# A graph layer on one core: segment sums in four column tiles with the fp32 one-hots stationary, an unrolled program, and layer norm statistics on VectorE

## What is computed

```python
N_NODES = 6250; F_X = F_E = F_OUT = 128; HIDDEN = 512      # 106,250 edges
h = jnp.maximum(_layernorm(x, axis=-1), 0.0)
agg = jax.ops.segment_sum(edge_attr, receivers, num_segments=N_NODES)   # receivers = dst, sorted
y = jnp.concatenate([agg, h], axis=1)
return x + jax.nn.relu(y @ W1 + b1) @ W2 + b2
```

## Time and profile before

| | |
|---|---|
| time, median of three runs | 326.34 us (325.3 to 327.11) |
| span of the profiled execution, first to last instruction | 320.9 us |
| what lies around that span, if the profiled execution took the median | 5.4 us |
| PE busy | 293.4 us, 91% |
| DVE busy | 287.6 us, 90% |
| POOL, ACT busy | 186.4 us and 127.8 us |
| bytes moved | 62.29 MB, mean 194 GB/s |

### The profile page before, as it was taken

The page is one execution under the profiler, slowest core; times in us unless marked ns, Lnnn a source line. Parts: engine busy times, 40 slices in busy tenths (PEclk is TensorE's granted clock), DMA queues, the critical chain, the costliest instruction groups (busy, mean ns, idle before and its releaser), DMA issues.

```text
span 320.9 us, 10106 instructions
## 1 busy us (share of the span) xinstructions
PE 293.4 (91%) x3270; PEld 289.1 (90%) x3270; DVE 287.6 (90%) x576; ACT 127.8 (40%) x430; POOL 186.4 (58%) x212
## 2 busy tenths in 40 slices
PE   1428999999999999999999999999999999999971
PEld 1327999999999999999999999999999999999961
DVE  5998999999999999999999999999999999993310
ACT  4140234443343543444444344354344443435240
POOL 4485374664676577577567567657756756742011
PEclk9999999999999999999999999999999999999997
DMA  6973657666666776775766666677586577400000
GB/s 199 390 276 93 219 157 236 229 213 210 221 215 219 217 241 189 235 253 149 290 223 200 216 222 209 214 229 252 168 267 236 158 257 237 140 3 16 17 18 27
DMA packets 30624, 62.29 MB, mean 194 GB/s; under 512 B 2042, under 2 KB 8936, under 8 KB 30608
## 3 DMA queue, kind: packets, MB, share of 16 engines
q1 hardware_dynamic: 29202, 60.79, 58.0%
q10 hardware_dynamic: 1406, 1.30, 1.2%
HBM read 58.88 MB, written 3.20 MB: 193 GB/s over the span
## 4 chain that ended last, share of the span: by engine, by line
PE 82%; issue 8%; DVE 4%; DMA 2%; POOL 1%; DVEq 0%; SPq 0%; POOLq 0%; ACT 0%
PE bank L833 21%; PE bank L790 19%; PE bank L847 13%; PE bank L804 9%; PE bank L802 9%; PE bank L803 9%; DMA hidden<-in_dst 2%; PE bank L814 2%; DVE low L234 1%; DVE rem L231 1%; POOL outrow L371 1%; DVE onehot L585 0%; DVE relT L647 0%; DVEq L627 0%; DVE colB L661 0%
## 5 line engine op out<-in xcount | busy, mean ns | idle before, releaser
L802 PE MATMUL bank<-onehot_h,edges 128*128 128x48 bf16 (+1 forms) x535 | 95.3, 233 | 3.7 <-DVE low L234 1.9
L804 PE MATMUL bank<-onehot_h,low 128*128 128x48 bf16 (+1 forms) x535 | 96.8, 237 | 0.0
L803 PE MATMUL bank<-onehot_h,rem 128*128 128x48 bf16 (+1 forms) x535 | 96.7, 235 | 0.0
L790 PE MATMUL bank<-onehot,edges 128*128 128x48 f32 x600 | 78.3, 280 | 4.7 <-DVE base_tab L678 4.0
L234 DVE TENSOR_TENSOR low<-rem 128x640 bf16<-128x640 f32 x84 | 82.4, 981 | 0.0
L790 PEld LDWEIGHTS bank<-onehot,edges 128*128 128x128 f32 x600 | 77.1, 203 | 5.0 <-issue 4.9
L231 DVE TENSOR_TENSOR rem<-edges 128x640 f32<-128x640 f32 x84 | 79.4, 945 | 0.0
L580 DVE TENSOR_TENSOR onehot_h<-relT_h,iota_h 128x240 bf16<-128x240 bf16 x107 | 73.7, 688 | 1.3 <-DVE base_tab L678 0.9
L802 PEld LDWEIGHTS bank<-onehot_h,edges 128*128 128x128 bf16 (+1 forms) x535 | 62.8, 117 | 5.5 <-issue 4.4
L495 ACT ACTIVATE hidden<-bank,b_col 128x256 f32<-128x256 f32 (+1 forms) x100 | 41.4, 467 | 63.9 <-PE bank L833 63.9
L804 PEld LDWEIGHTS bank<-onehot_h,low 128*128 128x128 bf16 (+1 forms) x535 | 62.4, 117 | 0.0
(11 more groups left out here) (79 smaller groups left out, 489.1 us busy)
## 6 DMA issues: line engine op xcount, KB each, us to landing
edges<-in_edge_attr SPq DMA_DIRECT2D x48, 640.0 KB, 4.1
edges<-in_edge_attr SPq DMA_DIRECT2D x23, 960.0 KB, 5.1
out_rows<-outrow SPq DMA_DIRECT2D x24, 128.0 KB, 1.7
xs<-in_x SPq DMA_DIRECT2D x21, 128.0 KB, 3.7
w<-in_L_gnn_W ACTq DMA_DIRECT2D x1, 512.0 KB
xs<-in_x ACTq DMA_DIRECT2D x1, 384.0 KB, 4.5
hidden<-in_dst SPq DMA_DIRECT2D x1, 320.0 KB, 3.5
edges<-in_edge_attr SPq DMA_DIRECT2D x1, 320.0 KB
```

The costliest lines, as they stand in the source:

```text
L790: ins = nc.tensor.matmul(sums_ps, edges[0:kp, slot, g * F:(g + 1) * F], onehot[0:kp, PLAIN.index(k), g, :], start=(g == 0), stop=(g == G - 1))
L802: nc.tensor.matmul(sums_ps, high[0:kp, cols], hot, start=(g == 0), stop=False)
L803: nc.tensor.matmul(sums_ps, middle[0:kp, cols], hot, start=False, stop=False)
L804: ins = nc.tensor.matmul(sums_ps, low[0:kp, i, cols], hot, start=False, stop=(g == G - 1))
```

## The change

The sums are made the other way round. The one-hot is now the stationary operand, 32 nodes wide, and the edges are the moving one, so a matmul gives 32 nodes by 128 features. A chunk has 384 edges (3 per partition), and four chunks form a round (`ROUND`, 1536 edges, 70 rounds with the remainder): chunk t of a round writes PSUM partitions 32t to 32t+31 of one bank. No edge is split any more; each of the 12 matmuls of a round is fp32. The sums come out untransposed, so ACT copies them to SBUF once a block (`copy_sums`), PE turns them (`turn_sums`, one transpose a round) and DVE adds four windows of 32 columns a round into `aggT` (`add_sums`). Blocks take 4, 3, 3, 3, 2 ... rounds, 65 in blocks 1 to 23. The layer norm's mean and variance come from two batch-norm instructions on DVE (`stats`), POOL makes the reciprocal root (`spread`), DVE adds `b2` (`add_b2`) and finishes the output rows straight from PSUM (`finish`). No engine has a loop on the way through the blocks.

```diff
-G = 5
+G = 3
 CHUNK = P * G
-W = 48
-SC = 7
+W = 32
+TILES = 4
+ROUND = TILES * CHUNK
+RING = 8
...
@@ POOL
+            def spread(b):
+                pool.wait_ge(stats_ready, b + 1)
+                nc.gpsimd.tensor_scalar(var[0:w, par, :], meanvar[0:w, par, :, 1], 1e-5, None,
+                                        ALU.add).then_inc(var_ready, 1)
...
+                nc.gpsimd.tensor_tensor(rstd[0:w, par, :], var[0:w, par, :], power[0:w, :], ALU.pow).then_inc(pow_ready, 1)
@@ ACT, the loop over blocks
+            for k in range(NB):
+                h_out(k)
+                if k >= 1:
+                    round_agg(k - 1, (k - 1) % 2, k - 1, chunks_by(k - 1))
+                copy_sums(k)
+                if k + 2 < NB:
+                    normalise(k + 2)
...
+                if k >= 1:
+                    relu(k - 1, (k - 1) % 2, k - 1)
@@ DVE
+            def stats(b):
+                for j in range(2):
+                    nc.vector.bn_stats(halves[0:w, par, j, :], xs[0:w, b, j * F:(j + 1) * F]).then_inc(halves_ready, 1)
...
+                for j in range(2):
+                    ins = nc.vector.bn_aggr(meanvar[0:w, par, j, :], halves[0:w, par, j, :])
+                ins.then_inc(stats_ready, 1)
+            def add_sums(k):
+                dve.wait_ge(sums_turned, k + 1)
+                for i, r in enumerate(ROUNDS[k]):
+                    cs = chunks_of(r)
+                    _, bases = nc.values_load_multi_w_load_instructions(
+                        base_tab[0:1, r * TILES:r * TILES + len(cs)], engines=[dve.engine], min_val=0,
+                        max_val=N - 1, skip_runtime_bounds_check_because="clamped when written")
+                    for j, c in enumerate(cs):
+                        if c:
+                            dve.wait_ge(agg_added, c)
+                        win = aggT[:, bass.ds(bases[j], W)]
+                        at = i * F + j * W
+                        nc.vector.tensor_tensor(win, turn_ps[:, at:at + W], win, ALU.add).then_inc(agg_added, 1)
+            for k in range(NB):
+                if k >= 1:
+                    add_sums(k - 1)
+                rest_of_h(k)
+                if k >= 1:
+                    rest_of_agg(k - 1, (k - 1) % 2, k - 1)
+                if k >= 3:
+                    finish(k - 3, (k - 3) % 2, k - 3)
+                if k + 2 < NB:
+                    stats(k + 2)
...
+                if k + 1 < NB:
+                    for r in ROUNDS[k + 1]:
+                        build(r)
+                    add_b2(k + 1)
@@ PE
+            def sum_rounds(k):
...
+                        for g in range(G):
+                            for t in range(TILES):
+                                e = t * G + g
+                                ins = nc.tensor.matmul(sums_ps[t * W:(t + 1) * W, cols], onehot[:, hots, e, :],
+                                                       edges[:, slot, e * F:(e + 1) * F], start=(g == 0),
+                                                       stop=(g == G - 1))
+            def turn_sums(k):
+                pe.wait_ge(sums_copied, k + 1)
...
+            for k in range(NB):
+                sum_rounds(k)
...
+                if k >= 1:
+                    layer1(k - 1, (k - 1) % 2, k - 1)
...
+                if k >= 2:
+                    layer2(k - 2, (k - 2) % 2, k - 2)
+                turn_sums(k)
+                if k + 1 < NB:
+                    turn_x(k + 1)
```

More of the change, by code:

```diff
@@ L401, in _ @@
[L401 to L413 removed]
+            nc.gpsimd.memset(ident[:, :], 0.0).then_inc(const_step, 1)
@@ L416, in _ @@
+            nc.gpsimd.tensor_copy(limit[:, :], limit_i[:, :]).then_inc(limit_ready, 1)
+            n = NWIDE * WIDE // CLEARS
+            for i in range(CLEARS):
+                nc.gpsimd.memset(aggT[:, i * n:(i + 1) * n], 0.0).then_inc(agg_cleared, 1)
+                if i < 2:
+                    spread(i)
+            for b in range(2, NB):
+                spread(b)
         @block.scalar
@@ L551, in _ @@
+            round_agg(NB - 1, (NB - 1) % 2, NB - 1, FULL + 1)
+            relu(NB - 1, (NB - 1) % 2, NB - 1)
             act.wait_ge(flag_ready, 1)
@@ L759, in _, with turn_ab @@
+                with dve.Fori(0, NB - 1) as b:
+                    rest_of_agg(NB + b, 0, b)
+                    finish(NB + b, 0, b)
+                rest_of_agg(2 * NB - 1, 0, NB - 1)
+                dve.wait_ge(out_summed, 2 * NB)
+                nc.vector.tensor_tensor(outrow[0:NLAST // 2, 0, :], out_ps[0:NLAST // 2, 0:2 * F],
+                                        xs[0:NLAST // 2, NB - 1, :], ALU.add).then_inc(out_added, 1)
         @block.tensor
         def _(pe):
-            def turn_rel(half, done):
+            def turn_ab(i, rel):
@@ L807, in turn_x, with turn_cd @@
-            def turn_x(b, par, first=False):
-                w = width(b)
+                    ins = nc.tensor.transpose(hid_ps[i][:, g * P:(g + 1) * P], rel[:, g:CHUNK:G], ident[:, :])
+                return ins
+            def turn_cd():
+                for g in range(G):
+                    nc.tensor.transpose(misc_ps[:, g * CC:(g + 1) * CC], relC[:, g:CHUNK:G], ident[0:CC, 0:CC])
+                for g in range(GR):
+                    ins = nc.tensor.transpose(misc_ps[0:KREST, 64 + g:65 + g], relD[0:1, g:REST:GR], ident[0:1, 0:1])
+                return ins
@@ new lines, in turn_sums @@
+            def turn_sums(k):
+                pe.wait_ge(sums_copied, k + 1)
+                if k >= 1:
+                    pe.wait_ge(agg_added, chunks_by(k - 1))
+                rows = W if k == NB - 1 else P
+                for i in range(len(ROUNDS[k])):
+                    ins = nc.tensor.transpose(turn_ps[:, i * F:i * F + rows], sums[0:rows, k % 2, i * F:(i + 1) * F],
+                                              ident[0:rows, 0:rows])
+                ins.then_inc(sums_turned, 1)
@@ L809, in turn_x @@
+            def turn_x(b):
+                w, par = width(b), b % 2
                 pe.wait_ge(xn_ready, b + 1)
-                if not first:
+                if b >= 1:
                     pe.wait_ge(hT_lo_ready, b)
```

940 lines of the change are left out of this document (402 added, 538 removed).

## The result

The changed kernel takes 338.3 us (median of four runs, 334.99 to 341.86) against 325.82 us for the kernel before on the same chip: a ratio of 1.031, with a 95% interval of 1.023 to 1.039. It is slower, where 317 us and faster was forecast; the time lies in the range. The profiled execution has a span of 333.4 us.

What follows compares the result with a forecast made beforehand. PE bounded the kernel before; afterwards a once-a-block chain through DVE, ACT and PE would. Start 36, 23 blocks of 11.4 us (262) and end 13 gave a 311 us span; 5.4 more made 317 us, range 302 to 373.

Steps and rivals of the forecast that it cites:

- start, to the end of `turn_sums`(1): Edges landing, one-hots, first sums and additions, and `layer1` at the lower clock: ends at 36 us (31 to 41).
- 23 blocks at the full clock: Blocks after the start, each set by the chain of additions, splits, layers and `turn_sums`: 11.4 us each, 262 in all.
- from there to the end: After the last `turn_sums`: the remaining layers, `relu` and drain, `finish` and the output store, 13 us.
- the price of a sum: PE's time for one new fp32 sum matmul, strips partly side by side: 0.119 us, 4.03 us a block.
- anything from 0.110 to 0.161 gives one time: Sum matmuls on PE costing 0.110 to 0.161 us each stay hidden behind the DVE and ACT part of the chain.
- Rival 3: PE's clock falls to 1.2 GHz in its 1.4 us waits: 15.8 us a block, time 418 us; chance 6%.
- The chain as the bound: A once-a-block loop through DVE's additions, the splits, both layers and `turn_sums` sets the time: 11.4 us a block; chance 55%.
- What was to be hidden: DVE's `finish`, `stats`, one-hots and `add_b2`, 3.2 us a block, fit beside PE's 5.5 us of `layer1` to `turn_sums`.
- Rival 1: Sum matmuls on the four strips don't overlap, so PE bounds at 13.9 us a block: time 371 us; chance 24%.
- PE bounds, and DVE keeps just ahead of it: Reading of the kernel before: PE 91% and DVE 90% busy, but PE holds 82% of the last-ending chain, DVE 4%.
- The 5.4 us between span and time: Amount by which the shown runs' median exceeds the profiled span, added to the 311 us span to give the time.
- rival 2: Longer DVE chain, from uncovered work or dear loads, or sums partly side by side: 12 to 13 us a block, 328 to 345; 10%.

## Why the prediction was wrong

Held against the span, where 311 was forecast (the second row is taken from the run with 20 idle matmuls, the third is what the changed kernel takes more):

| term | forecast | measured | difference |
|---|---|---|---|
| start, to the end of `turn_sums`(1) | 36 | 38.6 | +2.6 |
| 23 blocks at the full clock | 11.4 each | 10.7 each (245.9) | -16.3 |
| the clock | none | 281.4 - 245.9 | +35.5 |
| from there to the end | 13 | 13.4 | +0.4 |
| span | 311 | 333.4 | +22.2 |

- **The step that failed is the price of a sum, and with it the clock, which the sum put at nothing.** The prediction took 0.119 us a matmul, with the bf16 records as lower end at 0.110, and said that "anything from 0.110 to 0.161 gives one time". It is 0.053, under the lower end. For the chain that costs nothing, as the step says. But PE's wait is what the chain leaves over. The forecast had 1.4 us; by its own terms it is 11.2 - 9.5 = 1.7, since PE is free before the last transpose has drained. 33.9 sums at 0.066 less give 2.2 us more, and the stretch from `turn_sums` to `layer1` is some 0.6 shorter than forecast (5.4 instead of 6.0 in the mean block): 3.3, as measured (79.4 / 24). In such waits the clock fell, for 35.5 us in all, where the sum has no term for it. The prediction looked upwards, for the point from which dearer sums would make PE the bound, and downwards no further than to 0.110 and a wait of 2 us; a quarter of its own upper price, 0.238 / 4 = 0.060, never entered.
- **Rival 3, the clock falls in the waits, is what happened.** It had 6%, since "1.4 us is short beside that". That is sound: 15 idle matmuls give about this wait and lose at most 2.6 us. It should have been weighed at the wait that the cheapest sums would leave. Its price, 418 us, was too high: the clock comes back within each block, as the 10.9 and 13.6 us of the windows show, and does not fall in every wait.
- **The chain as the bound** was right: L702 waits for `agg_lo` in 24 blocks, and DVE and PE share the chain. PE has its half (52%); DVE with its queue and ACT have 32%, and 41% with the issue between their instructions, where half was forecast. Nearly each step was put slightly too dear: the load 0.36 us instead of 0.45, 0.51 across it instead of 0.61, and 0.87 from `turn_sums` to the first addition instead of 1.25. The distance of 0.32 was exact.
- **What was to be hidden was hidden.** One-hots take 0.543 us (0.56 forecast), the four batch-norm instructions 0.7 (0.8), and with the clock held up their place makes 1 us, 3 by the ratios.
- **Rival 1, strips that don't overlap,** had 24% and is out. The Trainium skill (TensorE: Matmul & The Clock Gate, What overlaps and what doesn't) lets a weight load overlap a running matmul only where the row group differs. These strips use all rows, and 72 loads and matmuls pass in 1.90 us, where whole-array fp32 records stand 0.105 to 0.119 apart: four times as dense, while the records of a single strip stand 0.109 apart. The measurement decides; it agrees with the "up to 4x" of the Trainium skill (TensorEngine Tiling, Theoretical Speedup).
- **"PE bounds, and DVE keeps just ahead of it"** was too simple: 0.9 us more of DVE's work a block (21.6 us in all) cost 14 us in the kernel before. It did not enter the sum.
- **Slips that did not decide.** The 5.4 us between span and time is 1.8 in the changed kernel (335.15 and 333.4 in one execution): the profiled execution of before was one of the faster ones, not the median. Rival 1's 13.9 us a block gives 369 + 5.4 = 374 us, not 371, and rival 2's 13 us gives 353, not 345.

## What to carry to other kernels

When a change takes work off the bound engine, work out its wait from the lowest price that the new work could have, and ask there what the clock does: 3.3 us of idling a block cost this kernel 35 us, more than the 25 that the change won with the clock held up. Take off the chain whatever need not be on it (loads ahead of the wait, independent matmuls in the gap, a second buffer) before the cheaper work is judged: the change that made this kernel 3% slower makes it 30% faster with `layer2` in the gap, two banks and the loads first. A gap that can't be closed is worth trying to fill with idle matmuls.

## What the runs showed of the hardware

- Fp32 matmuls with a 32-wide stationary operand on four strips in turn start 0.027 us a record; three in a row on one strip, 0.046 (3.30 us from first to last start of 72). The records of one strip stand 0.109 apart in either order.
- The longer PE idles once a block, the lower the granted clock, whether the wait is filled or cut: total waits at L702 of 79.4, 63.6, 50.2, 39.1 and 26.6 us go with 0.854, 0.904, 0.935, 0.974 and 0.987, and the other ways of shortening them fall near these (60.3: 0.91; 50.0: 0.924; 38.5: 0.968). Two things do not fit: 79.2 goes with 0.81, and the run with two banks, with 10.0 in all, has 0.977; its low slices lie in the first third, beside its two waits of 2.5 and 2.7 us.
- In the changed kernel a matmul of 256 columns takes 0.21 us at the lower level and 0.12 at the upper, and the falls come singly and in runs: blocks of one kind take 10.9 or 13.6 us with nothing in the program that tells them apart.
